# A state-space mixer with a mixture of experts: first stage and scan rebuilt by channel

## What is computed

```
x, z = split(einsum('bld,ed->bel', hidden, W_in))          # 256 channels each, by sequence
x = silu(causal_conv(x, conv_w, 4 taps) + conv_b)
k[h,l] = 2 Re sum_n Ct[h,n] exp(dt A[h,n] l)               # one kernel of 512 taps a channel
y = (causal_convolution(x, k) + D x) * silu(z)
h = layernorm(hidden + y @ W_out.T)
e = argmax(h @ gate_w.T + gate_b + expert_bias)            # top 1 of 8
out = layernorm(h + relu(h @ w1[e] + b1[e]) @ w2[e] + b2[e])
```

## Time and profile before

| what | us |
|---|---|
| runs (three) | 266.8, 268.2, 268.19 |
| median | 268.19 |
| span of the profiled execution | 263.8 |
| first dispatch on POOL | 141.89 |
| last dispatch begins | 188.43 |
| first store of a block | 190.42 |

### The profile page before, as it was taken

How to read it: one execution, slowest core, us unless ns; L and a number is a source line. 1 busy time by engine, 2 the same in 40 slices (tenths; PEclk the granted TensorE clock), 3 DMA queues, 4 the chain that set the end, 5 groups by cost and what they waited for, 6 DMA issues and landing times.

```text
span 263.8 us, 8892 instructions
## 1 busy us (share of the span) xinstructions
PE 239.2 (91%) x2763; PEld 215.1 (82%) x2764; DVE 177.0 (67%) x552; ACT 187.1 (71%) x528; POOL 139.8 (53%) x208
## 2 busy tenths in 40 slices
PE   8999979999999899999979999359989999999970
PEld 4888768888887678888869999349979999899960
DVE  1889995997218657777724878842877676566672
ACT  2999999856998778888655665207667777667740
POOL 6000000400009989999624687878746656657545
PEclk9999999999999999999999999759999999999995
DMA  7697884600399999999293221647865676677600
GB/s 232 180 313 288 346 334 150 244 0 0 105 310 332 310 279 296 308 320 302 66 361 120 93 93 41 212 92 191 220 179 172 200 210 164 203 195 208 189 34 6
DMA packets 54267, 52.06 MB, mean 197 GB/s; under 512 B 4415, under 2 KB 42817, under 8 KB 54114
## 3 DMA queue, kind: packets, MB, share of 16 engines
q1 hardware_dynamic: 51506, 46.65, 59.2%
q0 software_dynamic: 2304, 4.34, 4.6%
q10 hardware_dynamic: 432, 0.79, 0.8%
HBM read 38.14 MB, written 14.07 MB: 198 GB/s over the span
## 4 chain that ended last, share of the span: by engine, by line
PE 59%; DVE 10%; ACT 10%; POOL 9%; issue 6%; DMA 5%; SPq 1%; DVEq 0%; ACTq 0%; POOLq 0%
PE banks L1292 13%; PE banks L1477 9%; PE banks L1487 8%; PE banks L1370 7%; POOL dispatched_rows L568 5%; ACT BR L672 5%; PE banks L1380 5%; PE banks L1384 4%; PE banks L1275 3%; PE banks L1357 3%; PE banks L1435 2%; DMA X<-dispatched_rows 2%; POOL RE L558 1%; DMA out<-X 1%; POOL out L576 1%
## 5 line engine op out<-in xcount | busy, mean ns | idle before, releaser
L515 POOL TENSOR_TENSOR Wx<-BR,RE 128x384 f32 (+1 forms) x32 | 47.9, 1548 | 27.9 <-PE banks L1292 26.6
L1292 PE MATMUL banks<-Wx,XT 128*128 128x256 f32 x256 | 59.9, 380 | 1.7 <-ACT Z L643 1.7
L809 ACT ACTIVATE Z<-banks,BR 128x128 f32<-128x128 f32 x156 | 44.6, 368 | 18.4 <-PE banks L1477 18.3
L1292 PEld LDWEIGHTS banks<-Wx,XT 128*128 128x128 f32 x256 | 48.4, 190 | 9.0 <-issue 2.2
L576 POOL DMA_INDIRECT out<-X x39 | 38.4, 986 | 27.8 <-DVE X L1233 15.3
L1477 PE MATMUL banks<-Z 128*128 128x128 f32 x312 | 42.7, 281 | 0.4 <-ACT Z L798 0.2
L1487 PE MATMUL banks<-BR,Z 128*128 x312 | 41.1, 276 | 1.2 <-DVE X L1216 1.2
L1477 PEld LDWEIGHTS banks<-Z 128*128 128x128 f32 x312 | 39.0, 196 | 1.0 <-issue 0.5
L1487 PEld LDWEIGHTS banks<-BR,Z 128*128 128x128 f32 x312 | 37.8, 192 | 1.5 <-issue 1.5
L568 POOL DMA_INDIRECT dispatched_rows<-TR,CR x32 | 31.0, 970 | 9.3 <-POOL RE L558 9.3
L1057 DVE TENSOR_TENSOR X<-banks,Z 128x256 f32 (+1 forms) x32 | 20.4, 636 | 9.1 <-PE banks L1384 9.1
(11 more groups left out here) (220 smaller groups left out, 469.6 us busy)
## 6 DMA issues: line engine op xcount, KB each, us to landing
TR<-kernel_rows SPq DMA_DIRECT2D x32, 512.0 KB, 6.5
Z<-w SPq DMA_DIRECT2D x39, 256.0 KB, 3.1
dispatched_rows<-TR SPq DMA_DIRECT2D x3, 2310.0 KB, 8.8
X<-dispatched_rows SPq DMA_DIRECT2D x39, 66.0 KB, 2.1
XT<-hidden_t SPq DMA_DIRECT2D x10, 256.0 KB, 3.1
RE<-decay_and_turns SPq DMA_DIRECT2D x2, 1024.0 KB, 7.4
BR<-w SPq DMA_DIRECT2D x1, 2048.0 KB, 8.2
dispatched_rows<-TR SPq DMA_DIRECT2D x1, 1848.0 KB, 7.8
```

The lines of the kernel that those rows point to most:

```text
L515: nc.gpsimd.tensor_tensor(BC[:, k, 0:LAGS, :].rearrange("p m (s r n) -> p (m s) r n", s=STRIPS, r=2), Btab[:, :, :, :, :, one].rearrange(" ...
L809: last = nc.scalar.activation(HT[:, j, c * P:c * P + P], bank[UP_BANKS[j]][:, c * P:c * P + P], ACT.Relu, bias=B1[:, bass.ds(experts[j] * ...
L1292: last = mm(bank[X_BANKS[k]][:, j * CHAN:(j + 1) * CHAN], XT[:, slot, at:at + CHUNK], Wx[:, tap, :], start=(tap == 0), stop=(tap == TAPS - 1))
```

## The change

The first stage is rebuilt with channels on the partitions. PE projects x for one half of the channels and one batch at a time (a unit: 16 matmuls of 512 columns, the weights as the stationary side); ACT writes the last tap and the bias (`last_tap`), DVE adds the other three taps from PSUM (`add_taps`), PE turns the unit to tokens (`turn_x`), ACT applies silu on the copy out (`keep_x`). The gates come by channel and ACT applies silu at once. The powers of the decay are products of 16 fine and 8 coarse ones: DVE makes those of the first 16 groups, POOL, after the parameters, those of the second 16; POOL also makes the turning tables. Bias, taps and skip weights come in one small load.

In the scan, states are summed per group by plain powers (`sum_local`, four groups at a time) and turned between chunks by a small table (`turn_states`); their part is added to the convolution in the same bank (`add_states`). ACT copies the sum (`keep_y`) and two transfers from ACT's queue carry it back by channel (`send_y`, 64 KB each: 128 partitions of 128 columns at the source, 4 partitions with 32 runs of 128 columns at the destination), into a ring of 4 copies; the first 16 groups return to Y0, the others to Y1. POOL gates the first half in one operation, DVE the second half batch by batch, and the output projection takes the gated rows as they lie, so its transposes, copies and second loads of the hidden states are gone.

The dispatch slots are no longer filled ahead. Before blocks 8 to 11 are loaded, SP waits until the counts are final, reads eight row numbers from tables, and stores one block of empty rows behind each expert's last token: four, a wait until they have landed, then four.

The core of the diff:

```diff
-            filled = 0
-            for b in range(A_BATCH, BATCH):
-                turns = FILLS[b - A_BATCH]
-                sp.wait_ge(s_a, (b - A_BATCH) * 2 + 2)
-                load_batch(sp, b)
-                sp.dma_start(rows_of[:, filled:filled + turns, :],
-                             empties.unsqueeze(1).to_broadcast([P, turns, FILL_ROWS * ROW])).then_inc(s_fill, 16)
...
-            sp.wait_ge(s_kx, 3)
-            sp.dma_start(kext.rearrange("(j p) c -> p j c", p=P), Kx[:, :, :]).then_inc(s_kd, 16)
-            sp.wait_ge(s_kd, 16)
-            sp.wait_ge(s_fill, 16 * len(FILLS))
+            def store_rows(j):
+                sp.wait_ge(s_kx, 2 * j + 2)
+                sp.dma_start(kext[j * P:(j + 1) * P, :], Kx[:, j, :]).then_inc(s_kd[j], 16)
+                sp.wait_ge(s_kd[j], 16)
...
+            store_rows(0)
+            for g in range(T_SLOTS):
+                load_toeplitz(g)
+            store_rows(1)
+            for g in range(T_SLOTS, GROUPS):
+                load_toeplitz(g)
...
+                if g == EARLY_BLOCKS - 4:
+                    sp.wait_ge(s_last, 2)
+                    sp.wait_ge(s_ends, 2)
+                    starts = table_values(sp, ends, 0, EMPTY_ROW - P) + table_values(sp, ends, 4, EMPTY_ROW - P)
+                    for downwards in range(2):
+                        wait_past(sp, s_fill, downwards * 16 * (EXPERTS // 2))
+                        for e in range(downwards, EXPERTS, 2):
+                            sp.dma_start(slots_dram[bass.ds(starts[e], P), :], empty_block).then_inc(s_fill, 16)
...
+                    sp.wait_ge(s_empties, 16)
+                    sp.wait_ge(s_fill, 16 * EXPERTS)
...
-            def group_tables(r, k):
-                g = r * 2 + k
-                wait_apart(pool, s_s, g - 1)
-                one = bass.ds(g, 1)
-                falls = decay.rearrange("p m (s n g) -> p (m s) n g", s=STRIPS, g=GROUPS)[:, :, :, one].rearrange("p m n g -> p m (n g)")
-                nc.gpsimd.tensor_tensor(
-                    BC[:, k, 0:LAGS, :].rearrange("p m (s r n) -> p (m s) r n", s=STRIPS, r=2),
-                    Btab[:, :, :, :, :, one].rearrange("p m s r n g -> p (m s) r (n g)"),
-                    falls.unsqueeze(2).to_broadcast([P, LAGS * STRIPS, 2, PAIR * STATES]), ALU.mult).then_inc(s_bc, 1)
...
+            lagged = lambda table: table[:, :, FINE + COARSE:HALF_ANGLE]
+            each_lag = lambda a: a.unsqueeze(2).to_broadcast([P, GROUPS, LAGS])
+            tt(turn_parts[:, 0, :, :], lagged(cosine), each_lag(v(Z0)), ALU.mult)
+            tt(turn_parts[:, 1, :, :], lagged(sine), each_lag(v(Z1)), ALU.mult)
+            tt(turn_parts[:, 2, :, :], lagged(cosine), each_lag(v(Z1)), ALU.mult)
+            done(tt(turn_parts[:, 3, :, :], lagged(sine), each_lag(v(Z0)), ALU.mult))
+            tt(turned[:, :, :, 0], turn_parts[:, 0, :, :], turn_parts[:, 1, :, :], ALU.add)
+            done(tt(turned[:, :, :, 1], turn_parts[:, 2, :, :], turn_parts[:, 3, :, :], ALU.subtract))
...
+            def turning(part):
+                count = HALF * LAGS * 2
+                tt(Rot[:, part, :].rearrange("p g (m c) -> p (g m) c", c=FINE),
+                   turned[:, part, :, :].rearrange("p g m r -> p (g m r)").unsqueeze(2).to_broadcast([P, count, FINE]),
+                   same_state[:, :].unsqueeze(1).to_broadcast([P, count, FINE]), ALU.mult).then_inc(s_rot, 1)
+
+            turning(slice(0, HALF))
+            part = slice(HALF, GROUPS)
+            pool.wait_ge(s_far, 1)
+            expand(nc.gpsimd, Etab[:, part, :], part, first_coarse, cosine)
+            done(expand(nc.gpsimd, products[:, part, :], part, second_coarse, sine))
+            tt(Etab[:, part, :], Etab[:, part, :], products[:, part, :], ALU.add).then_inc(s_e1, 1)
+            turning(slice(HALF, GROUPS))
...
+            for k in range(Y_RING):
+                pool.wait_ge(s_yd[k], HALF // Y_RING * 32)
+            pool.wait_ge(s_z, BATCH)
+            tt(Y0[:, :], Y0[:, :], Z[:, 0:TOKENS], ALU.mult).then_inc(s_g0, 1)
...
-            def group_input(r, k):
-                g = r * 2 + k
-                wait_past(act, s_s, g - 1)
-                nc.scalar.activation(XG[:, k, :, :], X[:, bass.ds(g * GH, GH), :], ACT.Silu).then_inc(s_xg, 1)
...
+            def last_tap(u):
+                j = u // BATCH
+                act.wait_ge(s_x, u + 1)
+                wait_past(act, s_xtr, u - 1)
+                nc.scalar.activation(xc[:, u % 2, :], bank[u % 2], ACT.Identity,
+                                     scale=channel[:, j, TAPS - 1:TAPS], bias=channel[:, j, TAPS:TAPS + 1]).then_inc(s_x3, 1)
+
+            def keep_x(u):
+                j, b = u // BATCH, u % BATCH
+                act.wait_ge(s_xtr, u + 1)
+                nc.scalar.activation(x_chunks[:, j * P:(j + 1) * P, b, :], bank[2][:, :].rearrange("p (k c) -> p c k", k=CHUNKS),
+                                     ACT.Silu).then_inc(s_xe, 1)
...
+            def keep_y(g):
+                act.wait_ge(s_y, g + 1)
+                wait_past(act, s_yd[g % Y_RING], g // Y_RING * 32)
+                nc.scalar.activation(YT[:, g % Y_RING, :].rearrange("p (j u) -> p j u", j=2), backwards(6 + g % 2, CHUNK - 1, 2),
+                                     ACT.Copy).then_inc(s_yt, 1)
+
+            def send_y(g):
+                half, at = g // HALF, g % HALF
+                act.wait_ge(s_yt, g + 1)
+                for j in range(2):
+                    if half:
+                        home = bass.AP(X[:, :, :].tensor, (j * 64 + at) * CHAN * TILES, [[16 * CHAN * TILES, 4], [P, TILES], [1, P]])
+                    else:
+                        home = bass.AP(Y0[:, :].tensor, (j * 64 + at) * TOKENS, [[16 * TOKENS, 4], [P, TILES], [1, P]])
+                    act.dma_start(home, YT[:, g % Y_RING, j * P:(j + 1) * P]).then_inc(s_yd[g % Y_RING], 16)
...
+            act.wait_ge(s_rot, 1)
+            keep_local(0)
+            act.wait_ge(s_e1, 1)
+            keep_x(8)
+            last_tap(10)
+            for n in range(TURNS):
+                keep_y(4 * n)
+                if n:
+                    send_y(4 * n - 1)
+                if n + 1 < TURNS:
+                    keep_local(n + 1)
+                if n == 0:
+                    keep_rows(1)
+                    keep_powers(4)
...
+            def add_taps(u):
+                j = u // BATCH
+                dve.wait_ge(s_x3, u + 1)
+                for back in range(1, TAPS):
+                    if back > 1:
+                        dve.wait_ge(s_xk, u * LAGS + back - 1)
+                    stt(xc[:, u % 2, back:], bank[u % 2][:, 0:SEQ - back], channel[:, j, TAPS - 1 - back:TAPS - back],
+                        xc[:, u % 2, back:], ALU.mult, ALU.add).then_inc(s_xk, 1)
...
+            part = slice(0, HALF)
+            expand(nc.vector, Etab[:, part, :], part, first_coarse, cosine)
+            done(expand(nc.vector, products[:, part, :], part, second_coarse, sine))
+            tt(Etab[:, part, :], Etab[:, part, :], products[:, part, :], ALU.add).then_inc(s_e0, 1)
...
-                def project_x(j):
-                    chunk = k % 2 * 2 + j
-                    for tap in range(TAPS):
-
-                        at = chunk * CHUNK + tap
-                        last = mm(bank[X_BANKS[k]][:, j * CHAN:(j + 1) * CHAN], XT[:, slot, at:at + CHUNK], Wx[:, tap, :],
-                                  start=(tap == 0), stop=(tap == TAPS - 1))
-                    return last
...
+            def project_x(u):
+                j, b = u // BATCH, u % BATCH
+                wait_past(pe, s_xk, (u - 1) * LAGS)
+                pe.wait_ge(s_xt[b], 16)
+                mm(bank[u % 2], Win[:, j * P:(j + 1) * P], XT[:, b, :], start=True, stop=True).then_inc(s_x, 1)
...
+            def turn_x(u):
+                pe.wait_ge(s_xk, (u + 1) * LAGS)
+                wait_past(pe, s_xe, u)
+                for chunk in range(CHUNKS):
+                    at = slice(chunk * P, (chunk + 1) * P)
+                    last = nc.tensor.transpose(bank[2][:, at], xc[:, u % 2, at], ident[:, :])
+                last.then_inc(s_xtr, 1)
...
+            def add_states(g):
+                yt = bank[6 + g % 2]
+                pe.wait_ge(s_v, g + 1)
+                for j in range(2):
+                    last = mm(yt[:, j * P:(j + 1) * P], V[:, g % V_RING, j * 4:j * 4 + 4, :].rearrange("p h t -> p (h t)"),
+                              Etab[:, g, :], start=False, stop=(j == 1))
+                last.then_inc(s_y, 1)
...
-            def transpose_gated(s):
-                at = quad_of(s, 0)
-                if at:
-                    n, slot, batch = at
-                    for k in range(4):
-                        wait_past(pe, s_gt, n * 2 + (k // 2 - 1))
-                        for j in range(2):
-                            at = (k % 2) * 256 + j * P
```

(3 more changed lines are left out.)

1144 lines of the change are left out of this document (533 added, 611 removed).

## The result

The changed kernel takes 308.02 us (median of four runs, 304.65 to 311.11) where the kernel before took 267.5 on the same chip: a ratio of 1.141, interval 1.131 to 1.150, so some 38 us slower. The forecast had the sign and named the resource, but 281 was far too low, and 300, the end of the range, did not hold the time. The ratio goes by the two faster of the four runs (306.27 and 304.65) and the profile shown is of the slowest, 311.11 us (span 309.4), so a second profile of the same kernel, the repeat of number 5 with a span of 305.3, is set beside it where sizes matter.

What follows compares the result with a forecast made beforehand. Four DMA lanes carrying loads and returns were taken to bound the scan: 52 + 88.5 + 3 + 2.1 + 0.6 + 8.7 = 154.9 us to first dispatch, 13 later than before; span 276.8, plus 4.4 gives 281 us, range 252 to 300 (own 264 to 300).

Steps and rivals of the forecast that it cites:

- The share of a lane: Scan: four lanes carry 24 load and 32 return shares at 1.50 to 1.66 us each, 84 to 93, taken as 88.5 us.
- the end of the scan: From last return issued to landed: 3 us for W2 loads beside the returns plus 2.1 for landing, 5.1 us.
- the output stage: From the projection to the first dispatch: 8.7 us as before, behind a 0.6 us gate on DVE.
- emptied slots: Before blocks 8 to 11, SP's stores of empty rows: hidden by some 15 us of slack, costed nothing; 6 without it.
- The 4.4 us: Difference between the old kernel's span, 263.8, and its median time, 268.19; left as it is and added to the new span.
- The low end of the forecast's own range: POOL and lanes both at their low end, first dispatch at 140.9, some hand-over saved: 264 us.
- rival 3: Four lanes carry the returns, but POOL is quick, lanes run at 1.50, W2 disturbs nobody: 267 us; chance 0.09.
- what bounds the scan: Scan: returns dealt by four outer rows onto four of sixteen lanes, copies waiting for landings, groups about 2.8 us apart; chance 0.56.
- Rival 1: Scan: returns spread over all lanes and hide under PE, first dispatch at 125.4, whole 252 us; chance 0.25.
- Rival 2: Scan: ACT is held by issuing returns, 3.0 us a group, first dispatch at 159, whole 285 us; chance 0.10.
- 3 for W2: End of scan: W2 loads delay the last four groups' returns between 0 and 6 us, taken as 3.
- the first stage: Up to the first return, at 52 us: first half of x at about 40.5, POOL's second half of powers at 47.

Runs made afterwards that it cites:

- number 5: The changed kernel run once more with nothing altered, for a second profile; 304.51 us, ratio 1.136 to the kernel before.
- Numbers 6: Changed kernel with only one of each group's two returns sent, so half of the returned rows left out; 282.93 us, ratio 1.060 to the kernel before.
- 7: Changed kernel with each group stored to DRAM in one 128-row transfer and each half read back in eight 16-row reads; 305.37 us, ratio 1.146 to kernel before.
- 9: Changed kernel returning through DRAM by channel: four 32-row stores a group, 128-row reads, second half in eight pieces, W2 afterwards; 292.7 us, ratio 1.092 to kernel before.
- number 1: Changed kernel with the loads of W2, B1 and B2 waiting until every return has landed; 300.58 us, ratio 1.112 to the kernel before.
- numbers 11: Changed kernel returning through DRAM by channel, slots filled ahead in two and two transfers, 12 matmuls before the projection; 304.22 us, ratio 1.129 to 1.141.
- 12: Changed kernel with W2, B1, B2 after the returns, slots filled ahead by four fills, 14 matmuls before the projection; 293.44 us, ratio 1.095 to kernel before.
- number 4: Changed kernel with the same 64 returns issued from POOL's queue instead of ACT's, DVE gating the first half; 302.87 us, ratio 1.122 to kernel before.
- numbers 8: Changed kernel with 22 matmuls of 256 columns on PE between the last group and the projection; 305.72 us, ratio 1.146 to the kernel before.

## Why the prediction was right, and where it was wrong

The mechanism of the scan came out as forecast; the sum failed in its sizes. The share of a lane was priced too low (88.5 us for the scan, measured 99.4), the end of the scan was bounded too low (5.1, measured 14.4, 12.3 in the repeat), and two stages were carried over at the old kernel's time without a reason that holds in the new one: the output stage, and the expert stage with its emptied slots at nothing. The 4.4 us set between span and time are no part of this: in every run with both figures the time is 1.7 to 2.3 us above the span, the rest lay between the profiled execution of before and the median, and it cancels in the sum. The low end of the forecast's own range, 264, lies 3 us under what its sum gives (140.9, which is 267 in rival 3), and no row stands for the rest; the time lay beyond the other end.

**Right: what bounds the scan.** The forecast had the returns dealt out by their four outer rows, and the wait for landings in the place of PE and POOL. Numbers 6, 7 and 9 show it: a group falls from 3.56 to 2.43 us with half the returns, to 2.1 with one store of 128 rows (the eight groups ahead of the reads). Rival 1 (returns over all lanes, PE as the bound, 252) falls: PE works 37 of 56 us and stands waiting for ACT's copies, ACT for landings. Rival 2 (ACT held by issuing) falls as well: an issue costs mostly 0.54 us, and the two of a group, 1.1 to 2.8 us, are over before the landing for which the next copy waits. Rival 3 needed lanes at 1.50 us a share and falls with the 99.4.

**Wrong: the price of a share, 1.58 us for 56 shares.** Its upper end was 1.66, the rate of the loads before, and a group would have been 3.3 us at the most. It was 3.5 to 3.56, though three different loads of the lanes agree on 18 to 20 KB a us; over the 56 shares 99.4 us are 1.78 each (1.80 in the repeat). While four lanes carry both streams, each moves 18.0 KB a us against 19.3 before. Why it is 7% less stays open. A return's send stands behind the next copy in ACT's queue, so three groups are in flight, and 10.5 us of landing for three groups is 3.5 a group; but with never fewer than four packets in flight the landings are as long as the four lanes make them. The start is no better: from the second copy at 54.34 to the tenth at 84.16 eight groups take 3.73 each, beside the second half of x.

**Wrong: the end of the scan, 3 for W2 and 2.1 for a landing.** By number 1 a landing without W2 is 4.6 us, for the last returns still stand behind others in the same four lanes; the row of the kernel rows was of a transfer that had the lanes to itself. W2 and the biases are worth the other 9.6 (7.5 by the repeat). The forecast bounded W2 at 6, W2's own time on all lanes, as if the waits would only lie beside it; the last four groups of returns were still unissued or unlanded then, and went to the end of the same queues. ACT's last issues were held too (8.95 us for four).

**Wrong: the output stage, taken as before.** 8.7 was a row of PE at full clock. In the changed kernel PE has stood 16 us when the projection begins, and is granted 0.50 at first: 11.55 instead of 9.3, undone in numbers 11 and 12. The dispatches behind it also take 49.35 us from first to last, against 46.5 before (141.89 to 188.43) and 46.6 in numbers 11 and 12: between the fourth and the fifth lie 4.9 us in the changed kernel and 2.3 in number 12, so the second batch pays for the clock as well. With the 2.25 that is 5 us.

**Wrong: the emptied slots at nothing.** The 15 us of slack were read from a store that waits in POOL's queue. PE, however, needs the block's rows when it is through with block 7, and takes no block out of turn. The cost is near the 6 named as the price without that slack: PE stood 5.11 us, and from first to last store it is 5 us longer (3.7 in the repeat).

**Right in sum by luck, wrong in its parts: the first stage.** Forecast 52, measured 54.35 (52.67 in the repeat). POOL's powers were ready at 42.86 instead of 47, and x, at 45.9 instead of 40.5, was last. The timeline of POOL:

```profile
17.18 2.25 POOL L529 TENSOR_TENSOR EN<-EN 128x32 f32<-128x32 f32 x1
...
25.38 0.62 POOL L539 TENSOR_TENSOR Sel<-EN,mask 128x256 f32<-128x256 f32 x1
...
38.32 4.54 POOL L562 TENSOR_TENSOR CR<-CR,X 128x2048 f32<-128x2048 f32 x1
```

The wide passes cost 1.8 to 2.2 ns a column, not the 3.0 taken between DVE's rate and the 4.03 of the earlier trace rows. The Trainium skill, "GPSIMD Engine Reference", section "Elementwise — side-by-side cycle accounting", has 4497 ns for 2048 columns, and the 4.54 us here agrees: its figure was nearer than the row with its jumping operand. The other half went the opposite way. During DVE's three passes, 17 to 24 us, POOL's operations of 32 columns took 2.25 to 2.36 us each instead of 0.25; half of that standing aside was counted. So the selectors came at 26.0, PE waited 2.14 us for them, x was held up by 4.4 us on DVE, and a unit took 2.27 instead of 2.0.

## What to carry to other kernels

Price a transfer on the chip by its outer dimension: one with four outer rows, sent from ACT's queue, loads four lanes here, and these lanes' share of every other stream has to be added to it. A mean share of 0.67 says nothing about them; take bytes away and watch the pace, or count the packets in flight. Before a stage's time is carried over from the old profile, see what its engine did just before it, what is issued into its queues at that moment, and which in-order engine needs the result first: here a weight load, an idle PE and a store in the wrong queue cost 11 to 12 us together.

## What the runs showed of the hardware that was not expected

- The same transfer from POOL's queue showed a lane share of 1.15 where ACT's showed 0.67, at 191 and 185 GB/s, and landed in 6.7 to 7.1 us instead of 9 to 10 (number 4); more than four of its packets were in flight for 45% of the time, of ACT's for 1%.
- Reads to 16 neighbouring rows keep the lanes at a share of 1.27 and bring 102 GB/s (number 7), against 349 at a share of 1.14 in the earlier trace rows: a full share is no sign of bytes.
- PE began at half its clock after it had stood 5.04 us and at full clock after 1.22 us (numbers 8 and 12).
- A POOL operation on 32 columns took 2.25 to 2.36 us instead of 0.25 beside DVE passes over 2048 columns with two operands in SBUF.
